# Feature-interaction kernel: the 1 MB loads of x cut into four pieces of 32 partitions and spread over the sets

## The chip, the cores and the metric

One core of a Trainium2 chip runs the whole program. The metric is the device time of one execution in microseconds (us). Before the change it is 1306.55 us, the median of 3 runs (1305.3 to 1309.77).

## The reference

For each of 2048 batch entries there are 200 features of 64 numbers, in fp32. Each feature row is multiplied by a 64x64 matrix of its own, and the result is multiplied with all features of the same entry:

```python
# feature (2048, 200, 64), weight (200, 64, 64), out (2048, 200, 200), all float32
bilinear = jnp.einsum('bie,ied->bid', feature, weight)
out = jnp.einsum('bid,bjd->bij', bilinear, feature)
```

So 2048 x 200 x 64 x 4 bytes = 104.9 MB are read as features, and 2048 x 200 x 200 x 4 bytes = 327.7 MB are written as output; the weights are 3.3 MB and are loaded once.

## The kernel before, in words

The batch is cut into 16 blocks of 128 entries (n). Within a block there are two kinds of work.

Preparing a block: its features x lie in memory as 128 rows (one per entry, which becomes the partition) of 200 x 64 numbers. They are loaded in 7 loads per block into a buffer of two slots (`x`, XSLOTS = 2): six of 1 MB (128 partitions x 2 rows of 4096 bytes) and a small last one of 256 KB (128 x 2048 bytes). `load_x` (L204) issues one DMA per load from GpSimd's queue (L212, the small one L214). It waits until TensorE has transposed what lay in the slot two loads earlier. TensorE's `transposes(n, u)` (L248) turns half a load at a time (u = 0 to 12, 8 transposes of 128x128 each, 4 for the last) and waits for the load's arrival (`x_loaded`, L250); ScalarE stores the result into `xt` (L328). `bilinear(n, u)` (L259, matmuls L268) then applies the weights, and ScalarE stores that into `bl` (L338).

Scores of a block: 64 sets (s), each of two batch entries. A set is 16 matmuls of 64x200 (L286) into one of four PSUM tiles (`ps`); a copy "stages" the tile into the buffer `staging` (L316). Three of four sets are staged by ScalarE, and the set with s % 4 = 3 by VectorE. VectorE also prepares the operand `win` of every second set (L363, L370, L371). Four sets make an octet of 8 entries, which fills one of three slots of `staging` (OSLOTS = 3). When its four sets are staged, SyncE issues three stores of 400 KB (L189, 32 partitions each), and GpSimd's `store_rest` (L225, DMA in L231) a store of 50 KB for the four features that are left. Rows of output are 1600 bytes. A staging copy waits until the stores that last used its slot, three octets earlier, have landed (L312 to L315).

The order is written out by hand. While the scores of block n run, TensorE prepares block n + 1: after the scores of the set `transposed_at` = 2, 6, 11, 15, 20, 25, 29, 34, 38, 43, 48, 52, 57 come the transposes of u = 0 to 12, and three sets later the bilinear matmuls of the same u (L303 to L306). The four PSUM tiles are taken in turn by everything in the list `fillings`, so each filling waits for the copy out of the filling four places earlier (`wait_free`, L160).

GpSimd's queue runs in program order (L237 to L244): at set s it first issues `store_rest` if s ends an octet, which waits until all four sets are staged, and then a load if both halves of a slot's content have been transposed at s. The load issued at s = 52 of block n brings the first part of block n + 2, which the transposes of u = 0 need after the set s = 2 of block n + 1; the one issued at 57 is needed at 11, and those issued at 6, 15, 25, 34 and 43 are needed at 20, 29, 38, 48 and 57 of the same block.

Of the kernel before, what the change touches and what calls it, by code (L numbers as in the profile page):

```python
# [1 line left out]

# [5 lines left out]


def feature_interaction(nc, feature, weight, out):  # L10

# [7 lines left out]
    B, F, E = feature.shape  # L21
    NB = 128
    BLOCKS = B // NB
# [5 lines left out]
    NG = LINES // 2 + 1  # L29
    NX = NG // 2 + 1  # L30
    QUADS = CELLS
    PB = 2
    SETS_B = NB // PB
    XSLOTS = 2
    TILES = 4
    OCT = 8
    OSLOTS = 3
    WSLOTS = 4
    Z = 32
# [10 lines left out]
    def cells_of(u):  # L50
        return [8 * (u // 4) + u % 4, 8 * (u // 4) + u % 4 + 4] if u < NG - 1 else [LINES - 1]

    def quads_before(u):

        return max(ORDER.index(t) for t in cells_of(u)) + 1

    transposed_at = {60 * u // NG + 2: u for u in range(NG)}
    weighed_at = {s + 3: u for s, u in transposed_at.items()}
    assert all(s >= 2 * quads_before(u) - 1 for s, u in weighed_at.items())
    assert max(weighed_at) < SETS_B  # L60


    fillings = [("t", 0, 0), ("t", 0, 1)]
# [17 lines left out]
    with ctx:  # L81
        def sbuf(name, shape):
            return ctx.enter_context(nc.sbuf_tensor(name, shape, F32))

        def sem(name):
            return ctx.enter_context(nc.semaphore(name))

        w = sbuf("w", [128, FH, E])
        ident = sbuf("ident", [128, 128])
        x = sbuf("x", [128, XSLOTS, 2, 16 * E])  # L90
        xt = sbuf("xt", [128, CELLS, CELLS, C, R])
# [3 lines left out]

        ps = [ctx.enter_context(nc.psum_tensor(f"ps{q}", [128, 2, 512], F32)) for q in range(TILES)]

        w_loaded = [sem(f"w_loaded{i}") for i in range(NX)]
        x_loaded = [sem(f"x_loaded{i}") for i in range(XSLOTS)]
        ident_zero = sem("ident_zero")  # L100
# [16 lines left out]
        def tile_of(kind, n, i):  # L117
            return ps[number[kind, n, i] % TILES]

# [33 lines left out]
        def wait_staged(engine, s):  # L153

            if staged_by_dve(s):
                engine.wait_ge(staged_dve, s // 4 + 1)
            else:
                engine.wait_ge(staged_act, s // 4 * 3 + s % 4 + 1)

        def wait_free(engine, kind, n, i):  # L160

            at = number[kind, n, i]
            if at >= TILES:
                before, nb, ib = fillings[at - TILES]
                if before == "t":
# [35 lines left out]

        @block.gpsimd
        def _(pool):
            def load_x(at):  # L204
                n, u = at // NX, at % NX
                if at >= XSLOTS:
                    before = at - XSLOTS
                    pool.wait_ge(transposed, before // NX * NG + min(2 * (before % NX) + 2, NG))
                rows = feature_v[n * NB:(n + 1) * NB]
                if u < NX - 1:  # L210
                    halves = rows[:, 0:(NX - 1) * 32 * E].rearrange("b (a g i e) -> b a i g e", g=2, i=2, e=16 * E)
                    nc.gpsimd.dma_start(x[:, at % XSLOTS], halves[:, u // 2, u % 2]).then_inc(x_loaded[at % XSLOTS], 16)  # L212
                else:
                    nc.gpsimd.dma_start(x[:, at % XSLOTS, 0, 0:8 * E], rows[:, 2 * E * 3 * Z:F * E]  # L214
                                 ).then_inc(x_loaded[at % XSLOTS], 16)

            for u in range(XSLOTS):
                load_x(u)
            nc.gpsimd.memset(ident[:], 0.0).then_inc(ident_zero, 1)  # L219
            pool.wait_ge(ident_zero, 1)  # L220
            nc.gpsimd.affine_select(out=ident[:], in_=ident[:], compare_op=ALU.not_equal, fill=1.0,  # L221
                                    base=0, pattern=[[-1, 128]], channel_multiplier=1
                                    ).then_inc(ident_ready, 1)
            nc.gpsimd.memset(bl[:, 4 * C + 3:128:4, :], 0.0).then_inc(bl_cleared, 1)  # L224

            def store_rest(q):
                slot = q % OSLOTS
                b = q // (QUADS // 2) * NB + R * ORDER[2 * (q % (QUADS // 2))]
                for s in range(OCT // PB):
                    wait_staged(pool, OCT // PB * q + s)  # L230
                nc.gpsimd.dma_start(out_v[3 * Z:FH, b:b + OCT, :],  # L231
                                    staging[3:4 * C:4, slot].rearrange("p b h j -> p b (h j)")
                                    ).then_inc(rest_written[slot], 16)

            for u in range(XSLOTS, NX + XSLOTS):
                load_x(u)
            for n in range(BLOCKS):  # L237
                for s in range(SETS_B):
                    if PB * (s + 1) % OCT == 0:
                        store_rest((n * SETS_B + s) * PB // OCT)  # L240
                    if s in transposed_at and (transposed_at[s] % 2 or transposed_at[s] == NG - 1):
                        at = (n + 1) * NX + transposed_at[s] // 2 + XSLOTS
                        if at < BLOCKS * NX:
                            load_x(at)  # L244

        @block.tensor
        def _(pe):
            def transposes(n, u):  # L248
                at = n * NX + u // 2
                pe.wait_ge(x_loaded[at % XSLOTS], 16 * (at // XSLOTS + 1))  # L250
                wait_free(pe, "t", n, u)
                for g in range(len(cells_of(u))):
                    for c in range(C):
                        fs = slice(2 * E * (C * (u % 2) + c), 2 * E * (C * (u % 2) + c + 1))
                        last = nc.tensor.transpose(transpose_tile(n, u)[:, g, :, c, :],  # L255
                                                   x[:, at % XSLOTS, g, fs], ident[:])
                last.then_inc(transposed, 1)

            def bilinear(n, u):  # L259
                pe.wait_ge(xt_stored, n * NG + u + 1)  # L260
                if n == 0:
                    pe.wait_ge(w_loaded[u // 2], 64 if u < NG - 1 else 32)
                wait_free(pe, "b", n, u)
                for c in range(C):
                    for g, t in enumerate(cells_of(u)):
                        for h in range(2):
                            to = 64 * (h ^ g)
                            last = nc.tensor.matmul(bilinear_tile(n, u)[to:to + 64, g, c, :],  # L268
                                                    w[64 * h:64 * h + 64, C * t + c, :],
                                                    line_of_xt(n, t, c)[64 * h:64 * h + 64],  # L270
                                                    start=True, stop=True)
                last.then_inc(bilinear_done, 1)

            def scores(n, s):
                q = n * QUADS + s // 2
                if s == 0:
                    pe.wait_ge(bl_stored, (n + 1) * NG)
                if s % 2 == 0:
                    pe.wait_ge(win_filled, q + 1)
                wait_free(pe, "s", n, s)  # L280
                tile = tile_of("s", n, s)
                for b in range(PB):
                    r = PB * (s % 2) + b
                    for g in range(2):
                        for h in range(2):
                            last = nc.tensor.matmul(tile[64 * g:64 * g + 64, h ^ g, F * b:F * (b + 1)],  # L286
                                                    lines_of_bl(n, h, g, R * ORDER[s // 2] + r),
                                                    win[64 * h:64 * h + 64, q % WSLOTS, r, 1 - h:1 - h + F],
                                                    start=True, stop=True)
                last.then_inc(scores_done, 1)  # L290

            pe.wait_ge(ident_ready, 1)
            transposes(0, 0)
            transposes(0, 1)
            for u in range(NG):
                bilinear(0, u)
                if u + 2 < NG:
                    transposes(0, u + 2)
            pe.wait_ge(bl_cleared, 1)
            for n in range(BLOCKS):  # L300
                for s in range(SETS_B):
                    scores(n, s)
                    if s in transposed_at and n + 1 < BLOCKS:  # L303
                        transposes(n + 1, transposed_at[s])
                    if s in weighed_at and n + 1 < BLOCKS:
                        bilinear(n + 1, weighed_at[s])  # L306
# [97 lines left out]
```

## Time and profile before

| what | value |
|---|---|
| median of 3 runs | 1306.55 us |
| the profiled execution's own time | 1306.27 us |
| its span, first to last instruction | 1304.5 us |
| mean granted TensorE clock | 0.987 of full speed |
| busy: TensorE, ScalarE, VectorE, GpSimd | 92%, 81%, 71%, 19% of the span |
| moved by DMA | 439.58 MB, mean 337 GB/s |

In the profile PE is TensorE's matmuls, PEld its weight loads, ACT ScalarE, DVE VectorE, POOL GpSimd, SP SyncE; PEq, SPq and the like are the engines' own instruction queues. Times are in us from the start of the span unless marked ns. "A <- B: total, times, longest" in a list of waits says how long A sat idle until B released it. "[1.27 <-X]" at the end of a line of the timeline is the idle time of that engine before the line, and what ended it; "x64" is a number of instructions. In a table of windows each engine has its busy time in the window, then come the granted clock, the mean busy share of the 16 DMA engines (packets are counted where they begin, so it can pass 1) and the rate in GB/s.

### The profile page before, as it was taken

Reading aid. Unit: us, or ns where it says so; the run is one execution under the profiler, and the core shown is the slowest. Engines: PE = TensorE matmul, PEld = TensorE weight load, DVE = VectorE, ACT = ScalarE, POOL = GpSimd, SP = SyncE. Lnnn points to the kernel's source line nnn. Section 1 sums busy time; section 2 is a strip of 40 time slices with the busy share of each in tenths; the row PEclk is TensorE's granted clock in tenths of the full one; section 3 lists DMA queues with packets and bytes.
Section 4 is the critical chain, followed back from the end, with each engine's and each line's share of the span. In section 5 each row is a group of like instructions: output and inputs, shape, how many; then the busy total and the mean of one; then the engine's idle time right before and its main releaser. Section 6 shows DMA issues by size and latency. Waiting matters only on the chain.

```text
span 1304.5 us, 56312 instructions
## 1 busy us (share of the span) xinstructions
PE 1198.4 (92%) x24384; PEld 1030.4 (79%) x24384; DVE 925.6 (71%) x1792; ACT 1056.7 (81%) x1185; POOL 247.1 (19%) x375
## 2 busy tenths in 40 slices
PE   5999999999989999999989989899998999889985
PEld 4788788887778878897778878788777887778864
DVE  0477677777777768677776777777766777677795
ACT  4898787987889877997879977799787987779964
POOL 2111111122211112111121211212121112111111
PEclk9999999999999999999999999999998999999998
DMA  9699999999999999999999999999999999999899
GB/s 243 208 354 358 335 339 345 356 348 363 325 349 347 357 347 344 345 354 351 347 351 337 335 325 347 357 354 330 360 351 316 347 325 345 322 341 347 311 345 318
DMA packets 266133, 439.58 MB, mean 337 GB/s; under 512 B 40608, under 2 KB 237216, under 8 KB 265888
## 3 DMA queue, kind: packets, MB, share of 16 engines
q1 hardware_dynamic: 222112, 317.90, 69.6%
q0 software_dynamic: 43776, 118.09, 28.4%
q8 instruction: 194, 3.18, 1.0%
q14 instruction: 51, 0.42, 0.1%
HBM read 108.13 MB, written 327.68 MB: 334 GB/s over the span
## 4 chain that ended last, share of the span: by engine, by line
PE 66%; DMA 14%; issue 6%; DVE 5%; ACT 5%; SPq 2%; ACTq 0%; POOLq 0%; DVEq 0%
PE ps L286 43%; DMA out_dram<-staging 12%; PE ps L255 12%; PE ps L268 11%; ACT staging L316 3%; DVE staging L316 2%; SPq L189 2%; DMA x<-feature_dram 2%; ACT bl L338 2%; DVE win L363 2%; DVE win L371 1%; DMA w<-weight_dram 1%; DVE win L370 1%; ACT xt L328 0%; SPq L179 0%
## 5 line engine op out<-in xcount | busy, mean ns | idle before, releaser
L286 PE MATMUL ps<-win,bl 64*64 64x200 f32 x16384 | 840.2, 339 | 60.1 <-ACT staging L316 35.3
L286 PEld LDWEIGHTS ps<-win,bl 64*64 64x64 f32 x16384 | 674.5, 175 | 152.4 <-issue 58.8
L316 ACT COPY staging<-ps 128x800 f32<-128x800 f32 x768 | 625.8, 868 | 164.9 <-PE ps L286 67.6
L316 DVE COPY staging<-ps 128x800 f32<-128x800 f32 x256 | 253.2, 989 | 207.8 <-PE ps L286 206.4
L363 DVE COPY win<-xt 128x400 f32<-128x400 f32 x512 | 282.9, 553 | 138.5 <-ACT xt L328 78.0
L338 ACT COPY bl<-ps 128x1024 f32<-128x1024 f32 (+1 forms) x208 | 305.1, 1467 | 36.8 <-PE ps L268 35.3
L231 POOL DMA_DIRECT2D out_dram<-staging x256 | 161.6, 631 | 890.5 <-DVE staging L316 541.9
L268 PE MATMUL ps<-xt,w 64*64 64x128 f32 x6400 | 235.8, 275 | 13.8 <-issue 12.0
L255 PE MATMUL ps<-ident,x 128*128 128x128 f32 x1600 | 224.3, 283 | 21.4 <-DMA x<-feature_dram 15.5
L328 ACT COPY xt<-ps 128x1024 f32<-128x1024 f32 (+1 forms) x208 | 212.1, 1020 | 36.6 <-PE ps L255 36.2
L255 PEld LDWEIGHTS ps<-ident,x 128*128 128x128 f32 x1600 | 175.1, 143 | 73.5 <-issue 65.5
L268 PEld LDWEIGHTS ps<-xt,w 64*64 64x64 f32 x6400 | 203.4, 135 | 37.1 <-issue 20.1
L371 DVE COPY win<-win 64x400 f32<-64x400 f32 x512 | 202.9, 396 | 6.8
L370 DVE COPY win<-win 64x400 f32<-64x400 f32 x512 | 191.9, 375 | 16.0
L212 POOL DMA_DIRECT2D x<-feature_dram x96 | 71.0, 740 | 155.5 <-PE ps L255 152.8
L214 POOL DMA_DIRECT2D x<-feature_dram x16 | 11.0, 687 | 3.4 <-PE ps L255 3.4
L224 POOL MEMSET bl<- 128x3584 f32 x1 | 3.1, 3081 | 0.0
L328 ACT ACT_TABLE_LOAD x1 | 1.3, 1283 | 0.7 <-PEq L394 0.7
L221 POOL TENSOR_SCALAR_AFFINE_SELECT ident<-ident 128x128 f32<-128x128 f32 x1 | 0.3, 289 | 0.2 <-POOL ident L219 0.2
L219 POOL MEMSET ident<- 128x128 f32 x1 | 0.2, 224 | 0.0
L394 POOL MEMSET const-float32-0.0<- 128x1 f32 x1 | 0.1, 99 | 0.2 <-issue 0.2
L394 POOL MEMSET const-float32-1.0<- 128x1 f32 x1 | 0.1, 99 | 0.0
(2 smaller groups left out, 0.2 us busy)
## 6 DMA issues: line engine op xcount, KB each, us to landing
out_dram<-staging SPq DMA_DIRECT2D x768, 400.0 KB, 6.3
x<-feature_dram POOLq DMA_DIRECT2D x96, 1024.0 KB, 8.9
out_dram<-staging POOLq DMA_DIRECT2D x256, 50.0 KB, 5.8
x<-feature_dram POOLq DMA_DIRECT2D x16, 256.0 KB, 5.8
w<-weight_dram SPq DMA_DIRECT2D x24, 128.0 KB, 6.8
w<-weight_dram SPq DMA_DIRECT2D x2, 64.0 KB, 6.2
```

The source lines that it names most:

```text
L189: sp.dma_start(out_v[Z * z:Z * (z + 1), b:b + OCT, :], staging[z:128:4, slot].rearrange("p b h j -> p b (h j)")).then_inc(out_written[slot ...
L212: nc.gpsimd.dma_start(x[:, at % XSLOTS], halves[:, u // 2, u % 2]).then_inc(x_loaded[at % XSLOTS], 16)
L231: nc.gpsimd.dma_start(out_v[3 * Z:FH, b:b + OCT, :], staging[3:4 * C:4, slot].rearrange("p b h j -> p b (h j)")).then_inc(rest_written[slo ...
L255: last = nc.tensor.transpose(transpose_tile(n, u)[:, g, :, c, :], x[:, at % XSLOTS, g, fs], ident[:])
L268: last = nc.tensor.matmul(bilinear_tile(n, u)[to:to + 64, g, c, :], w[64 * h:64 * h + 64, C * t + c, :], line_of_xt(n, t, c)[64 * h:64 * h ...
L286: last = nc.tensor.matmul(tile[64 * g:64 * g + 64, h ^ g, F * b:F * (b + 1)], lines_of_bl(n, h, g, R * ORDER[s // 2] + r), win[64 * h:64 * ...
L316: copy(staging[:, slot, PB * s % OCT:PB * s % OCT + PB].rearrange("p b h j -> p h b j"), tile_of("s", n, s)[:, :, 0:PB * F].rearrange("p h ...
L328: nc.scalar.copy(group_of_xt(n, u), transpose_tile(n, u).rearrange("p g k c r -> p k g (c r)")).then_inc(xt_stored, 1)
L338: nc.scalar.copy(group_of_bl(n, u).rearrange(at), weighed.rearrange(at)).then_inc(bl_stored, 1)
L363: nc.vector.tensor_copy(win[:, q % WSLOTS, :, 1:F + 1:2].rearrange("p r (g c) -> p r g c", c=C), quad_of_xt(n, k).rearrange("p g c r -> p ...
L370: nc.vector.tensor_copy(win[64:128, slot, :, 0:F:2], win[0:64, slot, :, 1:F + 1:2])
L371: nc.vector.tensor_copy(win[0:64, slot, :, 2:F + 1:2], win[64:128, slot, :, 1:F + 1:2]).then_inc(win_filled, 1)
```

## The change: what it does

Each 1 MB load becomes four DMAs, piece 0 to 3, of 256 KB. Piece p takes partitions p, p + 4, p + 8, and so on. The small load stays one DMA. On GpSimd's queue the pieces of a load that stood at set s now stand at s + 1, s + 3, s + 5 and s + 7 (APART = 2), after the `store_rest` that may stand at the same set; the load that belongs to the last transposes of a block (u = 12, s = 57) is put off by 4 more sets, to 62, 64, 66 and 68. Each piece waits for the same transposes as the whole load did. TensorE's wait now counts the pieces of all loads of the slot. The first 9 loads, before the scores begin, are cut too, and their pieces are issued one behind the other. Stores are as before.

```diff
+    PIECES = 4
+    APART = 2
+    def pieces_of_load(at):
+        return PIECES if at % NX < NX - 1 else 1
+    loads_after = defaultdict(list)
+    for n in range(BLOCKS):
+        for s, u in transposed_at.items():
+            at = (n + 1) * NX + u // 2 + XSLOTS
+            if (u % 2 or u == NG - 1) and at < BLOCKS * NX:
+                for piece in range(pieces_of_load(at)):
+                    loads_after[n * SETS_B + s + 1 + 2 * APART * (u == NG - 1) + APART * piece].append((at, piece))
...
-            def load_x(at):
+            def load_x(at, piece):
...
+                batches = slice(piece, NB, pieces_of_load(at))
...
-                    nc.gpsimd.dma_start(x[:, at % XSLOTS], halves[:, u // 2, u % 2]).then_inc(x_loaded[at % XSLOTS], 16)
+                    nc.gpsimd.dma_start(x[batches, at % XSLOTS], halves[batches, u // 2, u % 2]
+                                        ).then_inc(x_loaded[at % XSLOTS], 16)
...
-            for n in range(BLOCKS):
-                for s in range(SETS_B):
-                    if PB * (s + 1) % OCT == 0:
-                        store_rest((n * SETS_B + s) * PB // OCT)
-                    if s in transposed_at and (transposed_at[s] % 2 or transposed_at[s] == NG - 1):
-                        at = (n + 1) * NX + transposed_at[s] // 2 + XSLOTS
-                        if at < BLOCKS * NX:
-                            load_x(at)
+            for s in range(BLOCKS * SETS_B):
+                if PB * (s + 1) % OCT == 0:
+                    store_rest(s * PB // OCT)
+                for at, piece in loads_after[s]:
+                    load_x(at, piece)
...
-                pe.wait_ge(x_loaded[at % XSLOTS], 16 * (at // XSLOTS + 1))
+                pe.wait_ge(x_loaded[at % XSLOTS], 16 * sum(map(pieces_of_load, range(at % XSLOTS, at + 1, XSLOTS))))
```

## Rows read from the trace of the kernel before

**Rows 1.** The page: busy, DMA share and rate in 40 slices, chain by engine.

```profile
PE 1198.4 (92%) x24384; PEld 1030.4 (79%) x24384; DVE 925.6 (71%) x1792; ACT 1056.7 (81%) x1185; POOL 247.1 (19%) x375
...
DMA  9699999999999999999999999999999999999899
GB/s 243 208 354 358 335 339 345 356 348 363 325 349 347 357 347 344 345 354 351 347 351 337 335 325 347 357 354 330 360 351 316 347 325 345 322 341 347 311 345 318
...
PE 66%; DMA 14%; issue 6%; DVE 5%; ACT 5%; SPq 2%; ACTq 0%; POOLq 0%; DVEq 0%
```

**Rows 2.** Waits over the whole span: us in total, times, longest.

```profile
ACT staging L316 <- issue: 48.5, 32, 3.8
ACT staging L316 <- DMA out_dram<-staging: 47.2, 27, 5.7
...
PE ps L286 <- ACT staging L316: 35.3, 28, 3.4
...
PE ps L255 <- DMA x<-feature_dram: 15.5, 4, 8.8
...
PE ps L255 <- ACT staging L316: 5.7, 6, 2.0
```

**Rows 3.** Windows of all engines: twelve us around a block's start, and most of the span.

```profile
590.00:602.00 12.00, 9.97 (x176) 8.25 (x179) 8.48 (x17) 7.49 (x11) 2.30 (x4) 1.00 1.03 380
...
70.00:1270.00 1200.00, 1126.56 (x23072) 969.75 (x23068) 885.02 (x1713) 995.36 (x1118) 228.25 (x346) 0.99 1.00 343
```

**Rows 4.** Timeline of the same block start, by engine: POOL, ACT, then PE.

```profile
595.51 0.85 POOL L231 DMA_DIRECT2D out_dram<-staging  x1 [3.69 <-DVE staging L316]
...
600.98 2.28 ACT L316 COPY staging<-ps 128x800 f32<-128x800 f32 x3 [2.47 <-issue]
...
596.20 3.35 PE L286 MATMUL ps<-win,bl 64*64 64x200 f32 x64 [0.24 <-ACT staging L316]
599.49 1.10 PE L255 MATMUL ps<-ident,x 128*128 128x128 f32 x8
601.85 2.41 PE L286 MATMUL ps<-win,bl 64*64 64x200 f32 x48 [1.27 <-ACT staging L316]
```

**Rows 5.** Waits in 9 us around block starts at 126.1 and 1157.2: one line each.

```profile
PE ps L286 <- ACT staging L316: 2.3, 1, 2.3
...
PE ps L286 <- ACT staging L316: 1.9, 1, 1.9
```

**Rows 6.** The line of the 1 MB loads, its landing time.

```profile
DMA to landing us min/median/max: 6.3/8.9/11.4
```

**Rows 7.** The line of the 256 KB loads: issue duration in ns, landing time.

```profile
L214 POOL DMA_DIRECT2D x<-feature_dram x16: 576/652/880, 38.6 to 1214.4; - x16
...
DMA to landing us min/median/max: 3.8/5.8/6.6
```

**Rows 8.** Windows of 1 us from the issue of one 256 KB load at 654.0.

```profile
654.00:655.00 1.00, 1.00 (x36) 0.93 (x32) 0.94 (x3) 0.89 (x2) 0.88 (x2) 1.00 1.06 373
655.00:656.00 1.00, 1.00 (x39) 0.95 (x32) 0.53 (x2) 1.00 (x2) 0.00 (x0) 1.00 1.02 333
656.00:657.00 1.00, 1.00 (x27) 0.66 (x17) 0.58 (x1) 1.00 (x2) 0.00 (x0) 1.00 1.10 281
657.00:658.00 1.00, 1.00 (x15) 0.83 (x11) 0.95 (x2) 0.31 (x1) 0.00 (x0) 1.00 0.97 353
658.00:659.00 1.00, 1.00 (x25) 0.92 (x28) 0.77 (x3) 0.42 (x1) 0.62 (x1) 1.00 1.03 389
```

**Rows 9.** Timeline, mid-block: the store that ends at set 39 (POOL), transposes of u = 10 (PE).

```profile
649.74 0.59 POOL L231 DMA_DIRECT2D out_dram<-staging  x1 [4.26 <-ACT staging L316]
...
656.96 1.09 PE L255 MATMUL ps<-ident,x 128*128 128x128 f32 x8
```

**Rows 10.** Windows by block, 15 blocks: the longest two, the shortest, the mean line.

```profile
675.70:759.00 83.30, 76.44 (x1529) 68.28 (x1529) 58.24 (x113) 72.30 (x75) 15.11 (x23) 0.98 1.00 343
759.00:834.80 75.80, 72.07 (x1533) 61.07 (x1528) 56.86 (x111) 61.30 (x74) 15.52 (x23) 1.00 0.99 336
991.40:1076.50 85.10, 77.99 (x1530) 69.59 (x1529) 58.54 (x115) 71.61 (x74) 15.08 (x23) 0.96 0.97 330
sum 1185.30, PE 1116.66 PEld 966.37 DVE 868.39 ACT 993.59 POOL 226.80; mean PE 74.44 PEld 64.42 DVE 57.89 ACT 66.24 POOL 15.12
```

More of the change, by code:

```diff
@@ L1 @@
+from collections import defaultdict
 from contextlib import ExitStack
@@ L211, in load_x @@
                     halves = rows[:, 0:(NX - 1) * 32 * E].rearrange("b (a g i e) -> b a i g e", g=2, i=2, e=16 * E)
-                    nc.gpsimd.dma_start(x[:, at % XSLOTS], halves[:, u // 2, u % 2]).then_inc(x_loaded[at % XSLOTS], 16)
-                else:
[L214 to L218, printed above, removed]
+                    nc.gpsimd.dma_start(x[batches, at % XSLOTS], halves[batches, u // 2, u % 2]
+                                        ).then_inc(x_loaded[at % XSLOTS], 16)
+                else:
+                    nc.gpsimd.dma_start(x[batches, at % XSLOTS, 0, 0:8 * E], rows[batches, 2 * E * 3 * Z:F * E]
+                                        ).then_inc(x_loaded[at % XSLOTS], 16)
+            for at in range(XSLOTS):
+                for piece in range(pieces_of_load(at)):
+                    load_x(at, piece)
             nc.gpsimd.memset(ident[:], 0.0).then_inc(ident_zero, 1)
@@ L233, in store_rest @@
                                     ).then_inc(rest_written[slot], 16)
-            for u in range(XSLOTS, NX + XSLOTS):
-                load_x(u)
-            for n in range(BLOCKS):
-                for s in range(SETS_B):
-                    if PB * (s + 1) % OCT == 0:
-                        store_rest((n * SETS_B + s) * PB // OCT)
-                    if s in transposed_at and (transposed_at[s] % 2 or transposed_at[s] == NG - 1):
-                        at = (n + 1) * NX + transposed_at[s] // 2 + XSLOTS
-                        if at < BLOCKS * NX:
-                            load_x(at)
+            for at in range(XSLOTS, NX + XSLOTS):
+                for piece in range(pieces_of_load(at)):
+                    load_x(at, piece)
+            for s in range(BLOCKS * SETS_B):
+                if PB * (s + 1) % OCT == 0:
+                    store_rest(s * PB // OCT)
+                for at, piece in loads_after[s]:
+                    load_x(at, piece)
         @block.tensor
```

## The prediction, made before the changed kernel was run

> **What bounds the kernel now.** I read the page first [rows 1]: TensorE is busy 92% of the span, the 16 DMA engines nearly all of it, and the chain that ended last lies on TensorE for 66% and on DMAs for 14%. So two resources are close to full, and the question is which one waits for the other, and where.
>
> The waits come next [rows 2]. ScalarE's staging copies waited 47.2 us for output stores, and 48.5 us for "issue". The second is a slot wait too, as the timeline of a block's start shows [rows 4]: PE had run the 64 matmuls of four sets by 599.55 (596.20 + 3.35), yet ACT begins to stage three of them only at 600.98, after 2.47 us of idle time; the scores were there and what the copy still lacked was its slot. Together 95.7 us, or 6.4 us in each of 15 blocks. TensorE sits idle 35.3 + 5.7 = 41.0 us behind those copies. Fresh x, on the other hand, hardly holds anything up: 15.5 us in 4 waits, of the start.
>
> The DMA engines are always occupied, but not always equally quick [rows 3]: in the 12 us around a block's start, with two loads of 1 MB in flight, they moved 380 GB/s, against 343 GB/s from 70 to 1270 us. So about 1 - 343/380 = 10% of their capacity is left over on the average, and the kernel loses time where a load and the stores meet. That is the stretch to look at: a load of 1 MB lands 8.9 us after issue, a small one of 256 KB 5.8 us [rows 6, 7].
>
> **The change, part by part.** I count from the profiled execution's own time, 1306.3 us (span 1304.5 and 1.8 around it), which is 0.3 us under the median of the runs.
>
> *Evening out (gain).* Bytes are the same; each 1 MB block of reading in front of the stores becomes 256 or 512 KB. It is not really "two sets apart": on GpSimd's queue only `store_rest` waits for sets, once in four, so pieces at s + 1 and s + 3 leave together whenever no octet ends between them. Going through the list, the 24 pieces of a block leave behind 14 of its 16 octets, one or two at a time. In the octets where a load now leaves, the stores should land earlier by what 512 KB take at 380 GB/s, 1.4 us, and later in others. Of the 95.7 us of slot waits, 14 block starts at 2.47 us take 35; 61 us lie elsewhere. I take half, 30 us, as gained. The bounds are 0 (the waits only move to other octets) and 61.
>
> *The block's start (loss).* Each piece is now issued late. The last piece of the load that stood at s = 52 stands at 59, behind the `store_rest` of set 59; its data are needed by the transposes after set 2, seven sets on. In the timeline [rows 4] that store's issue ends at 596.36 (595.51 + 0.85) and the transposes begin at 599.49: 3.1 us. A load of 256 KB, which is what a piece is, took 5.8 us to land (3.8 to 6.6) [rows 7], so the transposes come 2.7 us late (0.7 to 3.5). Behind them on TensorE stand all later sets; for them wait both copy engines and, in the end, the stores. Part of it is hidden: after these transposes TensorE already waits for a late staging copy, 1.27 us here; 11 of the 14 block starts have such a wait, 22.8 us in all [rows 5] (the first and the last of the 11 stand there), 1.6 us a block. If the slot comes free earlier, that wait goes and the wait for x takes its place. Net 2.7 - 1.6 = 1.1 us, x14 = +15 us. Bounds: 0, if that copy stays as late; 3.5 x 14 = 49 with no cover.
>
> *The other loads.* The tightest in mid-block is the load issued at 34: two pieces leave behind the store of set 39. That issue ends at 650.33, the second piece begins 0.65 us later [rows 7] at 650.98, and the transposes of u = 10 begin at 656.96 [rows 9]: 5.98 us against 5.8 us for landing, plus some for the piece ahead. I take 0.3 us x 14 = +4 us; 0 to 14.
>
> *Issuing.* 18 more DMAs per block on GpSimd, 0.65 us each [rows 7], are 12 us in 79, on an engine that is busy 19% [rows 1]: hidden. At 12 us of idle time in 79 it would still be hidden. Pieces also wait for transposes at most as long as whole loads did, so `store_rest` behind them is not later: 0. At the start of the program eight issues instead of two stand ahead of `ident` on the queue, some 4 us, but the first transposes wait for x anyway: 0, at most +4.
>
> *Beginnings of transfers (loss).* After a small load is issued the rate dips: 373, 333, 281, 353, then 389 GB/s in steps of 1 us [rows 8]. Against 373 that is 40 + 92 + 20 = 152 KB missing and 16 KB regained, 0.36 us of DMA time. There are 7 such beginnings in a block now and 15 afterwards (14 octets and the small load): 8 x 0.36 = 2.9 us, x14 = 40 us, if DMA is the bound throughout. With 10% of a block's 79 us left over, 7.9 us, it is mostly covered: I take +5, and keep 0 and 40 as ends.
>
> Sum: 1306.3 - 30 + 15 + 4 + 5 = 1300 us.
>
> **Rivals.**
> - *The block's start costs in full (slower).* If the last piece lands later than 3.1 + 1.6 = 4.7 us after its issue, the transposes after set 2 set the pace; where the evening out brings just a third of PE's waits away from block starts, (41.0 - 22.8)/3 = 6, the time is 1306 - 6 + 2.7 x 14 + 4 = 1342. For it: 3.1 us is under the shortest landing of 16 small loads, 3.8. Against it: TensorE already waits there.
> - *Beginnings of transfers (slower).* DMA counts in full: 1300 - 5 + 40 = 1335. For it speaks the dip; against it 380 GB/s with loads in flight. The Trainium skill (DMA: Bandwidth & Descriptors, Rules for kernel authors) asks for 128 partitions and at least 1 MiB per DMA for most bandwidth, which also speaks against cutting; by its fit of 2.0 us plus bytes over 436 GB/s (section Anatomy of one DMA) a piece takes an estimated 2.6 us and four in turn 6.0 us more than one load. The trace's 5.8 against 8.9 us is the same direction with a larger fixed part, but its landings overlap with others, so the 6 us are not paid as such.
> - *All blocks like the quick ones (faster).* Blocks last 75.8 to 85.1 us, 79.0 on the average [rows 10]. If slots never wait, all come near 76.5: -2.5 x 15 = -38, 1268 us. For it: PE's and ACT's busy time in a block, 74.4 and 66.2, leave room; against it the block's start.
> - *Waits only move (no change).* DMA engines stay occupied, one wait is replaced by another: 1306.
>
> **How the numbers follow.** Forecast 0.30, block's start 0.25, beginnings 0.12, quick blocks 0.20, only moved 0.13. A difference under 0.3% (4 us) can't be told from none here. Of the forecast two thirds fall under 1302.6 and the rest within 0.3%; quick blocks count as faster; the "moved" case spreads a third to faster, half to the same, the rest to slower. Faster 0.20 + 0.20 + 0.05 = 0.45; slower 0.37 + 0.01 = 0.38; the same 0.17. The term bounds alone span 1306 - 61 = 1245 to 1306 + 49 + 14 + 40 = 1409, but ends don't come together; the range goes from 1270 to 1338, inside both the quick-block and the block-start case, since cases of both signs hold most of the chance. The forecast's own range is 1290 to 1308.
>
> **What the profile would show.** Right: ACT's waits for slots near half of 95.7; a new wait of PE L255 for x, about one per block, 1 to 3 us, after the first three sets; staging behind it no longer late; landing of pieces 5 to 7 us; the stores' longest landing shorter. Wrong: no wait for x at block starts (the late piece costs nothing), or such waits at several places in a block; slot waits as long as before; or a rate below 343 GB/s with DMA engines full, which would make the beginnings the cause.

## The result

The changed kernel is slower: 1325.93 us, the median of 4 runs (1320.59 to 1330.56), against 1305.92 us (4 runs) of the kernel before. The ratio is 1.0156 with a 95% interval of 1.0100 to 1.0211. The time lies in the forecast range of 1270 to 1338 us, which was wide enough for losses too; but the forecast itself, 1300 us, was a gain, and what came was a loss.

The page of the changed kernel, which answers to [rows 1] (busy engines, DMA share in 40 slices, chain by engine and by line). Lines have moved: L306 are the matmuls of the scores, L275 the transposes, L336 the staging copies, L232 the pieces of x, L253 `store_rest`.

```profile
PE 1204.5 (91%) x24384; PEld 1038.7 (78%) x24384; DVE 922.8 (70%) x1792; ACT 1058.9 (80%) x1185; POOL 418.7 (32%) x663
...
DMA  9699999999999999999999999999999999999999
...
PE 44%; DMA 29%; DVE 7%; ACT 7%; issue 6%; SPq 3%; POOL 3%; ACTq 0%; POOLq 0%; DVEq 0%
PE ps L306 27%; DMA x<-feature_dram 19%; PE ps L275 10%; DMA out_dram<-staging 10%; PE ps L288 7%; ACT staging L336 5%; SPq L208 3%; DVE staging L336 3%; DVE win L383 2%; POOL out_dram L253 2%; DVE win L391 1%; ACT bl L358 1%; POOL x L232 1%; DVE win L390 1%; ACT xt L348 1%
```

The share of DMAs in the chain has doubled, from 14% to 29%, and 19% of the whole chain are now loads of x. The list of waits of the changed kernel says the same from TensorE's side (total, times, longest), beside [rows 2]:

```profile
PE ps L275 <- DMA x<-feature_dram: 76.3, 40, 10.0
...
ACT staging L336 <- DMA out_dram<-staging: 52.3, 36, 3.2
...
ACT staging L336 <- issue: 24.6, 18, 3.8
...
PE ps L306 <- ACT staging L336: 12.4, 15, 2.6
```

TensorE's wait for x rose from 15.5 us in 4 waits to 76.3 us in 40, and its wait for staging at the scores fell from 35.3 to 12.4 us. One wait took the place of the other, and the new one is larger. A block's start of the changed kernel shows where; it is the one of 14 with the longest wait (1.6 to 4.4 us, 3.1 on the mean). First the timeline of GpSimd, then that of TensorE:

```profile
604.99 0.62 POOL L253 DMA_DIRECT2D out_dram<-staging  x1 [3.91 <-DVE staging L336]
605.60 1.43 POOL L232 DMA_DIRECT2D x<-feature_dram  x2
```

```profile
604.44 3.75 PE L306 MATMUL ps<-win,bl 64*64 64x200 f32 x80 [0.23 <-DVE staging L336]
612.61 1.97 PE L275 MATMUL ps<-ident,x 128*128 128x128 f32 x8 [4.42 <-DMA x<-feature_dram]
614.50 4.01 PE L306 MATMUL ps<-win,bl 64*64 64x200 f32 x48
```

The last piece is issued at 605.60, behind `store_rest` of set 59. TensorE has done set 2 at 608.19 (604.44 + 3.75) and then sits for 4.42 us, until the piece has landed 7.0 us after its issue. And what comes next is slow: the eight transposes take 1.97 us where they took 1.10, the next three sets 4.01 us where they took 2.41 [rows 4]. The windows of the same stretch give the reason (PE, PEld, DVE, ACT and POOL, then granted clock, DMA share, GB/s):

```profile
602.00:605.40 3.40, 3.17 (x69) 2.89 (x67) 3.28 (x6) 3.29 (x4) 0.41 (x1) 1.00 0.95 334
605.40:608.80 3.40, 2.79 (x67) 2.20 (x60) 3.26 (x7) 2.77 (x4) 1.63 (x3) 1.00 0.97 281
608.80:612.20 3.40, 0.00 (x0) 0.00 (x0) 1.94 (x5) 0.35 (x1) 1.83 (x3) 0.87 1.04 378
612.20:615.60 3.40, 2.99 (x24) 2.41 (x28) 0.00 (x0) 0.99 (x1) 0.00 (x0) 0.50 0.95 306
615.60:619.00 3.40, 3.40 (x65) 2.74 (x60) 2.66 (x5) 1.26 (x3) 1.13 (x2) 0.63 0.54 202
619.00:622.40 3.40, 3.40 (x72) 2.77 (x68) 1.29 (x4) 3.09 (x4) 0.24 (x1) 1.00 0.96 312
```

After the wait the granted clock is 0.50, that is 1.2 of 2.4 GHz. Then the DMA engines run dry: 54% busy and 202 GB/s in the window from 615.6. In the timelines no set was staged between 609.14 and 616.18, so there was nothing new to store. In the kernel before, the stretch as far behind its transposes as this one (602.5 to 606.0 in the block of [rows 4]) moved 365 GB/s at a DMA share of 1.05.

The queue lines of the two pages (packets, MB, share of 16 engines' span) say the same of the whole span. First the kernel before, then the changed one:

```profile
q1 hardware_dynamic: 222112, 317.90, 69.6%
q0 software_dynamic: 43776, 118.09, 28.4%
```

```profile
q1 hardware_dynamic: 222112, 317.90, 68.2%
q0 software_dynamic: 48384, 118.11, 28.8%
```

With 1.1% on other queues in both, the DMA engines were without packets for an estimated 12 us before and 25 us in the change. That this can't be given back later, because the engines are full elsewhere, is argued and not measured by itself.

### The profile page after: what moved, and what is told of

Its sections match the earlier page's. It is cut to its first block, busy times and chain, and to the rows that moved or that the text cites. A ratio compares the mean times of both kernels' runs of the same rounds, so it can differ in the third digit from the quotient of the medians.

```text
span 1325.5 us, 56600 instructions
## 1 busy us (share of the span) xinstructions
PE 1204.5 (91%) x24384; PEld 1038.7 (78%) x24384; DVE 922.8 (70%) x1792; ACT 1058.9 (80%) x1185; POOL 418.7 (32%) x663
## 4 chain that ended last, share of the span: by engine, by line
PE 44%; DMA 29%; DVE 7%; ACT 7%; issue 6%; SPq 3%; POOL 3%; ACTq 0%; POOLq 0%; DVEq 0%
PE ps L306 27%; DMA x<-feature_dram 19%; PE ps L275 10%; DMA out_dram<-staging 10%; PE ps L288 7%; ACT staging L336 5%; SPq L208 3%; DVE staging L336 3%; DVE win L383 2%; POOL out_dram L253 2%; DVE win L391 1%; ACT bl L358 1%; POOL x L232 1%; DVE win L390 1%; ACT xt L348 1%
## 5 line engine op out<-in xcount | busy, mean ns | idle before, releaser
L306 PE MATMUL ps<-win,bl 64*64 64x200 f32 x16384 | 845.0, 343 | 32.2 <-ACT staging L336 12.4
L306 PEld LDWEIGHTS ps<-win,bl 64*64 64x64 f32 x16384 | 678.2, 177 | 127.4 <-issue 55.4
L336 ACT COPY staging<-ps 128x800 f32<-128x800 f32 x768 | 623.7, 864 | 165.3 <-PE ps L306 87.0
L253 POOL DMA_DIRECT2D out_dram<-staging x256 | 182.4, 712 | 848.0 <-DVE staging L336 415.4
L336 DVE COPY staging<-ps 128x800 f32<-128x800 f32 x256 | 252.6, 987 | 219.0 <-PE ps L306 217.7
L358 ACT COPY bl<-ps 128x1024 f32<-128x1024 f32 (+1 forms) x208 | 305.7, 1470 | 14.3 <-PE ps L288 12.5
L275 PE MATMUL ps<-ident,x 128*128 128x128 f32 x1600 | 231.5, 289 | 76.8 <-DMA x<-feature_dram 76.3
L275 PEld LDWEIGHTS ps<-ident,x 128*128 128x128 f32 x1600 | 180.0, 146 | 131.2 <-DMA x<-feature_dram 84.2
L348 ACT COPY xt<-ps 128x1024 f32<-128x1024 f32 (+1 forms) x208 | 210.2, 1011 | 77.4 <-PE ps L275 76.9
L232 POOL DMA_DIRECT2D x<-feature_dram x384 | 223.6, 584 | 42.4 <-PE ps L275 38.7
L288 PE MATMUL ps<-xt,w 64*64 64x128 f32 x6400 | 230.1, 273 | 1.3 <-issue 0.6
L235 POOL DMA_DIRECT2D x<-feature_dram x16 | 10.5, 655 | 8.6 <-PE ps L275 8.6
L348 ACT ACT_TABLE_LOAD x1 | 1.3, 1283 | 0.7 <-PEq L414 0.7
```

The lines of the kernel that those rows point to most:

```text
L232: nc.gpsimd.dma_start(x[batches, at % XSLOTS], halves[batches, u // 2, u % 2]).then_inc(x_loaded[at % XSLOTS], 16)
L253: nc.gpsimd.dma_start(out_v[3 * Z:FH, b:b + OCT, :], staging[3:4 * C:4, slot].rearrange("p b h j -> p b (h j)")).then_inc(rest_written[slo ...
L336: copy(staging[:, slot, PB * s % OCT:PB * s % OCT + PB].rearrange("p b h j -> p h b j"), tile_of("s", n, s)[:, :, 0:PB * F].rearrange("p h ...
L348: nc.scalar.copy(group_of_xt(n, u), transpose_tile(n, u).rearrange("p g k c r -> p k g (c r)")).then_inc(xt_stored, 1)
L358: nc.scalar.copy(group_of_bl(n, u).rearrange(at), weighed.rearrange(at)).then_inc(bl_stored, 1)
```

## The experiments

Each ratio is to the kernel before, run alongside, with its 95% interval. Two theories stood against each other at the start. A: the last piece of one load comes too late at each block's start. B: every beginning of a transfer costs DMA time, wherever it stands.

| run | what | us | ratio |
|---|---|---|---|
| change | all loads cut and spread | 1325.93 | 1.0156 (1.0100 to 1.0211) |
| e1 | only the block-start load cut and spread | 1344.97 | 1.0286 (1.0235 to 1.0336) |
| e2 | all but the block-start load | 1297.31 | 0.9940 (0.9914 to 0.9966) |
| e3 | cut, not spread | 1296.93 | 0.9939 (0.9913 to 0.9965) |
| e4 | change, TensorE kept busy in the wait | 1311.45 | 1.0040 (1.0010 to 1.0070) |
| e5 | APART = 1 | 1301.82 | 0.9973 (0.9946 to 0.9999) |
| e6 | spread as far as there is room | 1298.91 | 0.9951 (0.9922 to 0.9981) |
| e7 | e1, TensorE kept busy | 1335.52 | 1.0230 (1.0194 to 1.0265) |
| e8 | before, with the same extra matmuls | 1308.57 | 1.0026 (0.9997 to 1.0054) |
| e9 | before, 16% fewer bytes stored | 1267.79 | 0.9692 (0.9666 to 0.9717) |
| e10 | e3, 32 neighbouring partitions a piece | 1382.20 | 1.0580 (1.0556 to 1.0604) |
| e11 | e3, eight pieces | 1338.45 | 1.0249 (1.0223 to 1.0275) |
| e12 | change, 16% fewer bytes stored | 1284.12 | 0.9822 (0.9792 to 0.9851) |

**e1: only the load for the block's start.**

```diff
-        return PIECES if at % NX < NX - 1 else 1
+        return PIECES if at % NX == 0 else 1
...
-  loads_after[n * SETS_B + s + 1 + 2 * APART * (u == NG - 1) + APART * piece].append((at, piece))
+  loads_after[n * SETS_B + s + (1 + APART * piece) * (at % NX == 0)].append((at, piece))
```

> Only the load that the transposes after set 2 of the next block need (the one that stood at s = 52) is cut and spread; the other loads stay whole at their old places. Theory A, the late last piece at the block's start costs the time: PE waits for x about 40 us in all before the transposes of u = 0, PE's waits for staging after them (22.9 us before) are gone, half clock after most block starts; 1306 + 18 = about 1324 us. Theory B, each beginning of a transfer costs DMA time, whatever its place: only 2 of the 8 added bursts of a block are left, about 1306 + 5 = 1311 us, spread evenly.

It came out slower than the change itself, 1345 us; B expected 1311 and falls. A had 1324, so it has the place right and the size too small. The timelines show why (GpSimd, then TensorE): the next load, still whole, now stands ahead of the last piece on the queue (it is the last of the three DMAs of the first line), and the piece lands after 7.5 us (613.70 to 621.23; 6.7 to 8.1 at the 14 block starts). The waits before the transposes of u = 0 come to 66.6 us, added up from the timeline, where about 40 were expected.

```profile
607.63 1.82 POOL L232 DMA_DIRECT2D x<-feature_dram  x3
613.08 0.63 POOL L253 DMA_DIRECT2D out_dram<-staging  x1 [3.62 <-DVE staging L336]
613.70 0.88 POOL L232 DMA_DIRECT2D x<-feature_dram  x1
```

```profile
621.23 1.87 PE L275 MATMUL ps<-ident,x 128*128 128x128 f32 x8 [4.96 <-DMA x<-feature_dram]
```

**e2: all loads but that one.**

```diff
-        return PIECES if at % NX < NX - 1 else 1
+        return PIECES if 0 < at % NX < NX - 1 else 1
...
+  loads_after[n * SETS_B + s + (1 + 2 * APART * (u == NG - 1) + APART * piece) * (at % NX > 0)].append((at, piece))
```

> The complement: the load for the block's start stays whole at s = 52, all others are cut and spread as in the change. Theory A: the wait for x at block starts is gone, the staging wait there is back; about 10 us of x waits of u = 2, 4, 8, 10 stay: 1306 to 1314 us, full clock at block starts. Theory B: 6 of 8 added bursts stay, about 1306 + 15 = 1321 us. If the evening out of the other loads brings what the prediction said, it would show here alone: under 1290 us.

1297 us: with one load of seven put back, the whole loss is gone and 0.6% is gained. The waits of this run:

```profile
ACT staging L336 <- DMA out_dram<-staging: 49.0, 35, 3.6
...
ACT staging L336 <- issue: 38.0, 32, 4.6
...
PE ps L275 <- DMA x<-feature_dram: 31.0, 26, 8.5
PE ps L306 <- ACT staging L336: 28.6, 31, 2.9
```

Some 16 us of the x waits are those of the start that were there before; the rest are the loads with seven to nine sets of room, before u = 8 and u = 10. The evening out did not bring the 1290 us or less: slot waits of ACT are 87 us, hardly less than the 95.7 of before.

**e3: cut, but issued together where the whole load stood.**

```diff
-  loads_after[n * SETS_B + s + 1 + 2 * APART * (u == NG - 1) + APART * piece].append((at, piece))
+  loads_after[n * SETS_B + s].append((at, piece))
```

> All loads are cut in four, but the pieces are issued one behind the other where the whole load stood (last piece some 2 us after the first). Theory A: cutting costs nothing, within 0.5% of before, 1300 to 1312 us, no x wait of PE behind the first block. Theory B, if a beginning is paid by each piece: 18 more a block at 0.36 us, 14 blocks, up to 90 us more if DMA is the bound, and some 1320 to 1340 us if it is half covered.

Cutting costs nothing; it gains 0.6% and comes out just under A's 1300 to 1312 us. B falls a second time, for pieces of 256 KB: 18 more DMAs a block and no more DMA time (see below). ACT's slot waits are even longer here than before, and the kernel is quicker all the same:

```profile
ACT staging L336 <- issue: 56.7, 41, 3.9
ACT staging L336 <- DMA out_dram<-staging: 56.3, 30, 5.3
```

**e4, e7, e8: TensorE kept busy in the wait.** The matmuls of set 2 are done four times, in the change, in e1, and in the kernel before as a control.

```diff
-                for b in range(PB):
+                for b in [b for _ in range(4 if s == 2 and n + 1 < BLOCKS else 1) for b in range(PB)]:
```

> The change as it is, and TensorE does the 16 matmuls of set 2 of each block but the last four times instead of once (the same result is written again), some 2.1 us of work in a stretch in which it would wait for x some 3 us. If a good part of the loss is the half clock that follows the wait (81 us at half clock against 37), the clock stays full after block starts and 1326 falls to about 1316 us. If the clock does not matter, or the later staging of set 2 costs as much, the time stays at 1326 us or rises by up to 10 us.

> The kernel with only the block-start load cut and spread (1345 us, 93 us at half clock), with the 16 matmuls of set 2 done four times in each block but the last. If the half clock after the wait is a large part of the loss, the clock stays full and the time falls by 15 to 25 us to 1320 to 1330 us; if the wait alone costs, it stays at 1345 us or above.

> Control: the kernel before with the same repeated matmuls. Here PE has no wait for x to fill, only 1.6 us a block for staging behind it. The added work, 2.1 us in 15 blocks, can't gain: 1306 us if that wait covers most of it, up to 1330 us if nothing does. If it came out under 1300 us, the gain of the repeated matmuls would have nothing to do with the wait for x.

The extra matmuls do not bring the piece earlier; they fill part of the wait (43.6 us before the transposes of u = 0 in the change, 17.9 in e4, added up from the timelines), and what they change is the clock. Mean granted clock of the change and of e4:

```profile
core 0: 1325.5 us, clock 0.970
```

```profile
core 0: 1313.4 us, clock 0.989
```

At two levels, 0.970 means 2 x 0.030 x 1325.5 = 80 us at half clock, and 0.989 29 us. The ratio falls from 1.0156 to 1.0040, that is to 1311 us where about 1316 were expected, and the control came out as expected, at 0.3% more (interval -0.03 to 0.54%). So by these values more than half of the loss of the change came with TensorE at half clock after its wait; by the intervals the fall of 1.2% is known to 0.6% either way. In e7 the clock rises from 0.966 to 0.982, and 1.0286 becomes 1.0230: some 7 us, less than the expected 15 to 25, with about 48 us at half clock left. There the wait is longer and 2.1 us of work do not fill it. In e1 and e7, then, the larger part of the loss is not shown to come from the clock.

**e5, e6: spread with room.** e5 sets APART to 1. e6 pulls in the three loads that had waits (the one for the block's start, and those needed before u = 8 and u = 10) and leaves the others as in the change:

```diff
+    LATER = {11: (1, 1, 3, 3), 12: (5, 7, 9, 11), 1: (1, 3, 5, 7), 3: (1, 3, 5, 7), 5: (1, 2, 3, 3), 7: (1, 1, 1, 1), 9: (1,)}
...
+  loads_after[n * SETS_B + s + LATER[u][piece]].append((at, piece))
```

> The change with APART = 1: the pieces of a load stand at s + 1 to s + 4, the last load's at 60 to 63. Every last piece then stands at least 10 sets ahead of its use, instead of 7 to 9. Theory A (lateness): the waits of PE for x at u = 0, 4, 8, 10 (57 us) are gone, time under before's, about 1295 us as with cutting alone. If spreading itself were harmful, whatever the room, it would stay near 1310 us.

> Spread as far as the room allows: the load for the block's start leaves behind the stores of sets 51 and 55 only, those of s = 25 and 34 behind 23, 27 and 35, the others as in the change. Theory A: no x waits of PE in mid-block and at block starts, and the staging wait at block starts gone too (3.4 us in the run with that load whole): 1297 - 14 = about 1283 us. Rival: waits only move; the slot waits come back where the x waits go, and it stays at 1295 to 1300 us.

In e6 the x waits are nearly gone, and at block starts the staging wait stays away too (4.6 us in all ahead of set 3, added up from the timeline, against 22.9 before). The time, 1299 us, is that of cutting alone: the rival of this run, that waits only move, was right, and my 1283 us wrong. Waits of e6:

```profile
ACT staging L336 <- DMA out_dram<-staging: 54.3, 38, 2.9
...
ACT staging L336 <- issue: 38.5, 34, 2.6
...
PE ps L306 <- ACT staging L336: 21.7, 32, 1.3
PE ps L275 <- DMA x<-feature_dram: 21.5, 10, 9.2
PE ps L306 <- issue: 15.1, 19, 2.0
```

The longest slot wait has halved, from 5.7 to 2.9 us; the total, 92.8 against 95.7 us, is nearly the same. e5, 1302 us, is between, and short of the 1295 expected: no x waits behind the program's start, little gain. There the transposes waited for staging copies instead, 17.6 us in 15 waits.

**e9, e12: fewer bytes stored.** Every third store writes only half of its columns, in the kernel before and in the change: 16% of the stored bytes, 12% of all bytes moved.

```diff
-  sp.dma_start(out_v[Z * z:Z * (z + 1), b:b + OCT, :], ...
+  cols = F if z == 2 else 2 * F
+  sp.dma_start(out_v[Z * z:Z * (z + 1), b:b + OCT, 0:cols], ...
```

> The kernel before, but the third of the three stores of an octet writes only the first 200 of its 400 columns (rows of 800 instead of 1600 bytes), so 52 of 440 MB are left out of the output; everything else is as it was. Theory C, the DMA engines' work sets the pace and waits only move about (which is why evening out brought nothing): the time falls by most of the 12% of bytes until PE and ACT are the bound, to 1200 to 1240 us, slot waits mostly gone. Rival: the pace is set by PE and ACT with their block-start waits, and DMA only looks full: 1290 to 1305 us.

> The change as it is, with the same half of the columns of every third store left out of the output as in the kernel before with fewer bytes. Theory A: the last piece is late by its place in the order, so PE still waits for x at block starts, 1.5 to 3 us in each, and the time is 20 to 30 us above that of the kernel before with fewer bytes. Rival: the wait for x comes from full DMA engines; with 12% less traffic it goes, and both have the same time within 5 us.

e9 gained 40 us; its 1268 lies between the 1200 to 1240 of theory C and the 1290 to 1305 of the rival. Queue lines of its page:

```profile
q1 hardware_dynamic: 222112, 265.47, 62.2%
q0 software_dynamic: 43776, 118.09, 30.8%
```

Shares times spans: 1278 us of engine time before, 0.930 x 1258.3 = 1170 us now, 108 us less, for 40 us of time. So the DMA engines' work does hold the kernel before back, but something else holds it after some 40 us; what that is was not tested. In e12 the waits for x at block starts are as long as ever with 12% less traffic (46.1 us against 43.6 in the change, added up from the timelines; none in e9), and 1284 stands 16 us above 1268: A again, its expected 20 to 30 us a little too high. The late piece is late by its place in the order: with 12% less traffic it stays late, and with an earlier place, in e5 and e6, it does not. The DMA engines are still 93% busy in e12, so that a piece would be late beside idle engines too is not shown.

**e10, e11: how a load is cut.** e3 with pieces of 32 neighbouring partitions, and with eight pieces of 16 partitions.

```diff
-  batches = slice(piece, NB, pieces_of_load(at))
+  batches = slice(piece * NB // pieces_of_load(at), (piece + 1) * NB // pieces_of_load(at))   # e10
-    PIECES = 4
+    PIECES = 8                                                                                  # e11
```

> Cutting alone, but a piece takes 32 neighbouring partitions instead of every fourth. If which partitions a piece takes matters (every fourth keeps the spread of a whole load), this loses the 0.6% that cutting alone brought or more: 1305 us and above. If only the size of a DMA matters, it is equal to cutting alone: 1297 us.

> Cutting alone, into eight pieces of 16 partitions (every eighth), issued one behind the other where the whole load stood, the last some 4 us after the first. If finer pieces are what brought 0.6%, a little more: 1290 to 1297 us. If each beginning costs, or GpSimd's issuing (36% busy or more) begins to hold up the stores behind it: 1300 to 1315 us.

Queue q0, which carries x, in e3, e10 and e11:

```profile
q0 software_dynamic: 48384, 118.11, 28.2%
```

```profile
q0 software_dynamic: 48384, 118.11, 32.8%
```

```profile
q0 software_dynamic: 54528, 118.13, 30.8%
```

Shares times spans (1294.2, 1381.8 and 1332.3 us) are 365, 453 and 410 us of engine time for the same bytes; the kernel before has 0.284 x 1304.5 = 370. Against e3 that is +88 and +45 us, and the times are 85 and 42 us longer. With the stores, which also took longer for the same bytes, it is +111 and +53 us, so some 0.8 us of time for each us of added DMA time. This is the other half of what e9 showed: upwards the DMA engines are the bound.

e10 fell on the side that it was to fall on if partitions matter, much further than expected. A piece of e10 also reads other rows of `feature` than a piece of e3, neighbouring instead of every fourth; that rival was not tested. e11 lies above both of its expected ranges, and it has two differences from e3 at once: twice as many DMAs of half the size, and 16 partitions instead of 32. Which of them costs the 45 us is not shown, so theory B is refuted for pieces of 256 KB only.

## Why the prediction was wrong, point by point

*Evening out (gain): this step failed.* "I take half, 30 us, as gained." Slot waits of ACT fell by 19 us, from 95.7 to 76.9, and in e2 and e6, where hardly a piece is late at a block's start, by 9 and 3 us; e6, evened out and with room, is no quicker than e3, which is not evened out at all and has longer slot waits (113.0 us) than the kernel before. So the term was worth nothing that these runs show, where 30 us were taken. The mistake was to take a slot wait for a loss of its own. The DMA engines have the same bytes to move however they are ordered, and the copy that waits less at one place waits at another: the case "Waits only move", to which I gave 0.13, was true for this term. Without it the recorded sum is 1306.3 + 15 + 4 + 5 = 1330 us; that 1326 lies so near is partly luck, as the other terms were off too.

*The block's start (loss): right place, too small.* Foreseen were 2.7 us late, of which 1.6 replace the old staging wait. Added up from the timeline over the block starts, TensorE's idle time before the transposes of u = 0 is 43.6 us (3.1 in each of 14), and the old wait after them, 22.9 us, is gone: +21 us instead of +15. The last pieces landed in 5.8 us on the mean (4.2 to 7.0; the 7.0 is the block shown), just as foreseen; but TensorE stood ready 2.7 us after their issue, not 3.1. What the step did not price at all is the half clock behind the wait, 80 us of it in place of 2 x 0.013 x 1304.5 = 34. The transposes above took 1.97 us at half clock and 1.10 at full, so 46 us more at half clock can add an estimated 23 us of work at most. By the values of e4 and its control it made more than half of the loss.

*The other loads: right in kind.* The tight ones were that before u = 10, as worked out, and that before u = 8; the idle time before the mid-block transposes of u = 2 to 10 is 14 us in all, against +4 and an upper end of 14. Waits at several places in a block stood among the signs of being wrong.

*Beginnings of transfers: no loss.* +5 was taken and 40 kept as an end. e3 has 18 more DMAs per block, and q0's engine time is 365 against 370 us; in the change it is 382. The dip behind a small load [rows 8] is real but is not an added cost; whole loads have their own slow stretch (317 GB/s from 2 to 4 us after the issue of one at 642.4). The Trainium skill's rule for most bandwidth, at least 1 MiB per DMA (DMA: Bandwidth & Descriptors, Rules for kernel authors), speaks against cutting. The trace of e3 does not bear it out for this case: four times 256 KB take no more engine time than 1 MB.

*Issuing: right as to time.* GpSimd is busy 32% instead of 19%. It now stands in the chain, with 3%, and did not before; but that is the issues of stores and of late pieces, and no run separates how long they take from where they stand.

TensorE's own account shows where the 21 us of added span lie. These are its groups on the page before and on the page after (busy us, mean ns of one, then the idle time before them):

```profile
L286 PE MATMUL ps<-win,bl 64*64 64x200 f32 x16384 | 840.2, 339 | 60.1 <-ACT staging L316 35.3
L268 PE MATMUL ps<-xt,w 64*64 64x128 f32 x6400 | 235.8, 275 | 13.8 <-issue 12.0
L255 PE MATMUL ps<-ident,x 128*128 128x128 f32 x1600 | 224.3, 283 | 21.4 <-DMA x<-feature_dram 15.5
```

```profile
L306 PE MATMUL ps<-win,bl 64*64 64x200 f32 x16384 | 845.0, 343 | 32.2 <-ACT staging L336 12.4
L275 PE MATMUL ps<-ident,x 128*128 128x128 f32 x1600 | 231.5, 289 | 76.8 <-DMA x<-feature_dram 76.3
L288 PE MATMUL ps<-xt,w 64*64 64x128 f32 x6400 | 230.1, 273 | 1.3 <-issue 0.6
```

Idle time rose by 55.4 us before the transposes and fell by 27.9 before the scores and by 12.5 before the bilinear matmuls; busy time rose by 6.1 (1198.4 to 1204.5). Together that is 21.1 us. The waits for x thus cost more than the waits that they replaced. Busy time rose by less than the 23 us that the half clock could have added at most, so this account alone does not show the clock's part; that rests on e4.

Three versions beat both kernels: the loads spread only as far as they have room (e6), all but one spread (e2), and only cut (e3). They take 1297 to 1299 us, 0.5 to 0.6% less than the kernel before, and can't be told apart. Why cutting gains 0.6% is open. In e3 q0's engine time is 5 us less than before, but in e2, as quick, it is 4 us more (0.290 x 1290.6 = 374). On TensorE the idle time before the bilinear matmuls is 5.6 us in e3 against 13.8 before, which is the size of the gain, but no run says why it is less.

## What to carry to other kernels

Before a transfer is moved later, count for each piece the time from the instruction that lets it go to the one that needs it, with landing time in a full queue, and price the clock behind the wait as well as the wait. In this kernel, whose DMA engines are full, evening out moved waits and did not shorten the time; less work for the DMA engines did (e9), and more work made it longer (e10, e11). And how a load is cut over the partitions can matter more than when it is issued: 5.8% in e10, 1.6% in the change.

## What the runs showed of the hardware that was not expected

Which partitions a DMA takes: 32 neighbours cost 453 us of engine time for x, every fourth 365, and 16 partitions eight apart 410. The Trainium skill (SBUF — State Buffer, Door 1: The DMA port swizzle) says that bandwidth depends on how many of 16 ports the partitions reach, and that 32 neighbouring partitions reach 8. By the table there, every fourth partition reaches all 16 and every eighth only 8. The trace agrees in that every fourth is cheapest; the ports do not tell 453 from 410, as both cuts reach 8, and e11 differs in size and number of DMAs as well. No run here shows the ports themselves.

The clock after a wait: after 12 of the 14 waits for x at block starts of the change (2.2 to 4.4 us) the granted clock was 0.50 for a part of the work that followed, as in the windows shown; after the other two, of 1.6 and 2.9 us, it stayed at 1.00. The Trainium skill (TensorE: Matmul & The Clock Gate, HAM oscillation — how this bites in real kernels) describes the same pattern, a wait for a DMA and work at the lower clock behind it; the trace agrees.
